# Another order on every engine, and other PSUM banks, in a four-layer graph network

## The chip, the cores and the metric

The kernel runs on one core of a Trainium2 chip. The metric is device time in microseconds of one execution; the time before is the median of three runs.

## The reference

The input `x` has 32 items of 512 nodes with 256 features, and all items share one 512 x 512 adjacency matrix `adj` (a sixteenth of it set). Four layers follow each other, each of the form `x = x + layer(relu(layernorm(x)))`, all in float32:

```python
# layer 0: dense attention over neighbours, one head of 256
e = leaky_relu((h @ W1) @ (h @ W2).T, 0.2); a = softmax(where(adj > 0, e, -1e12))
out = relu(a @ (h @ W3))
# layers 1 and 3: graph attention (GAT), 4 heads of 64
q = h @ W; e = leaky_relu(e_src[i] + e_dst[j], 0.2); a = softmax(where(adj > 0, e, -9e15))
out = elu(a @ q)
# layer 2: multi-head attention, 4 heads of 64, masked by adj, then @ Wo + bo and a layer norm
out = layernorm((softmax(mask(Q K^T / 8)) @ V) @ Wo + bo) * gamma + beta
```

## The kernel before

Nothing goes back to memory between the layers. The program is a software pipeline written out by hand: `first` does layer 0 and the front of layer 1 of item 0, then `slots` runs a list of *slots*. In one slot three items are in flight: item `a` is in layer 0 and the front of layer 1, item `b` (one older) in the rest of layer 1 and the front of layer 2, item `c` in the rest of layer 2 and in layer 3. Every engine (PE for matmuls and transposes, DVE, ACT, POOL, and SP for DMAs) has a `slot` function that lists its steps in the order in which that engine takes them, strictly one after the other. What one engine hands to another goes through a semaphore (`Signal`). There are 33 slots after `first`; in the first and in the last two of them one or two of the items are missing.

The names that matter here, all of them steps of one item:

- `transposed(w, layer, t)` on PE: the normalised activations `hn` are transposed, one of four row blocks, and ACT copies them out (`h_transposed`).
- `u_columns`, `scores0`, `v_rows`, `weights_transposed0`, `aggregate0`: layer 0 on PE; DVE does `masked_max0` and `lrelu0`, ACT the exponentials `exp0`; `relu0` (ACT), `residual0` (POOL) and the next statistics (DVE) close it.
- `q_rows`, `gat_max_across`, `gat_max_spread`, `gat_rows`: front of a GAT layer. `gat_rows_out` (DVE) leaves one row per head and block in `growT`; SP's `spread` writes it to DRAM and reads it back broadcast over 128 partitions (`r_loaded`), and only then can DVE make the weights, `gat_weights(w, g, h, *ts)`, that PE's `gat_aggregate(w, g, h)` needs with POOL's `gat_values`.
- `qk_columns`, `scores2`, `masked_max2`, `exp2`, `weights_transposed2`, `weights_out2`, `inverse_spread`, `aggregate2(w, p)`, `norm2`, `o_rows`, `o_out`: layer 2.
- `idle_turns(bank, count)`: matmuls of the identity into an unused bank, which stand in the thinly filled slots.

PSUM has eight banks; `BANK` says into which of them each stage writes. A stage may write a bank only when its former contents were copied out; where the order alone doesn't guarantee that, PE has a wait in its list, such as `masked0.wait(pe, a, 3)` ahead of `transposed(c, 3, 0)`. PE uses its array in three shapes: whole (128 x 128), half the columns (`gat_aggregate` and `aggregate2`, 128 x 64) and half the rows (`scores2`, 64 x 128).

## Time and profile before

| | |
|---|---|
| median of three runs | 2945.29 us (2944.38 to 2945.89) |
| profiled execution | span 2943.7 us; this plus 1.6 us is the median |
| instructions | 68275, of them 27732 matmuls and as many weight loads |
| granted TensorE clock, mean over the span | 0.997 of full speed |
| length of a full slot | 88.7 us |

The profile gives for each engine the time in which it was busy. Float32 matmuls appear as two instructions each, and they are pipelined: the start of one group to the start of the next says what a group costs, the duration of an instruction does not.

### The profile page before, as it was taken

The page shows a single profiled execution, that of the slowest core. Times are in us where ns is not written, and L with a number is a line of the kernel's source. Part 1 is how long each engine was busy: PE and PEld are TensorE (multiplying, and loading weights), DVE is VectorE, ACT ScalarE, POOL GpSimd, SP SyncE. Part 2 cuts the span into 40 slices and gives each one's busy share as a digit, 9 for nine tenths or more (in the row PEclk, how much of TensorE's full clock was granted, in tenths as well). Part 3 has the DMA queues.
Part 4 walks back from the last instruction along what each step waited for, and adds up shares of the span by engine and source line. Part 5 has one row for each costly group of instructions (what it writes and reads, how often), then busy time and mean ns, then how long its engine had stood idle before and what let it go on. Part 6 is the DMA issues. An engine that isn't in the chain of part 4 may idle for free.

```text
span 2943.7 us, 68275 instructions
## 1 busy us (share of the span) xinstructions
PE 2887.3 (98%) x27732; PEld 2034.8 (69%) x27732; DVE 2127.5 (72%) x5596; ACT 1682.3 (57%) x3554; POOL 827.8 (28%) x917
## 2 busy tenths in 40 slices
PE   7899999999999999999999999999999999999998
PEld 5566767666767666767667767667767667776766
DVE  5576787776787776877776877776877777877764
ACT  2555655655656655656655656656656656656543
POOL 2123222323222323222233232233222233222221
PEclk9999999999999999999999999999999999999999
DMA  3001011101011101011101011101011111011010
GB/s 102 22 23 45 27 41 45 44 23 45 23 44 45 44 23 44 23 44 44 38 30 44 23 45 44 37 30 44 23 45 44 34 33 40 28 37 37 17 36 30
DMA packets 58840, 109.89 MB, mean 37 GB/s; under 512 B 5568, under 2 KB 41408, under 8 KB 58528
## 3 DMA queue, kind: packets, MB, share of 16 engines
q1 hardware_dynamic: 58032, 104.61, 10.8%
q8 instruction: 220, 3.60, 0.5%
q0 software_dynamic: 496, 0.92, 0.3%
q14 instruction: 92, 0.75, 0.1%
HBM read 88.21 MB, written 17.30 MB: 36 GB/s over the span
## 4 chain that ended last, share of the span: by engine, by line
PE 77%; DVE 12%; POOL 6%; issue 2%; ACT 1%; SPq 0%; DMA 0%; POOLq 0%; DVEq 0%; ACTq 0%
PE ps L972 19%; PE ps L1080 11%; PE ps L1106 8%; PE ps L1115 8%; PE ps L978 8%; PE ps L1142 8%; PE ps L1029 8%; PE ps L958 4%; DVE stats L641 3%; POOL rstd L367 3%; POOL xc L417 3%; DVE pB L753 2%; PE ps L1017 2%; DVE nb L658 1%; DVE hn L829 1%
## 5 line engine op out<-in xcount | busy, mean ns | idle before, releaser
L389 POOL TENSOR_TENSOR qx<-qx,xc 128x512 f32<-128x512 f32 x128 | 163.7, 1279 | 869.4 <-ACT qx L529 869.4
L641 DVE BATCH_NORM_STATS2 stats<-xc 128x6 f32<-128x256 f32 x384 | 134.7, 413 | 328.6 <-POOL xc L399 264.1
L448 ACT ACTIVATE hn<-xc,nb,rstd 128x256 f32<-128x256 f32 x384 | 209.1, 592 | 163.9 <-DVE nb L658 160.7
L1080 PEld LDWEIGHTS ps<-vals,pA 128*64 128x64 f32 x8192 | 253.9, 138 | 54.6 <-issue 54.5
L972 PE MATMUL ps<-wgat,hT 128*128 128x264 f32 x1024 | 267.4, 395 | 1.8 <-ACT hT L457 1.8
L1080 PE MATMUL ps<-vals,pA 128*64 128x65 f32 x8192 | 266.4, 223 | 2.1 <-DVE pA L753 2.0
L1080 PE MATMUL ps<-vals,pB 128*64 128x65 f32 x8192 | 264.0, 223 | 0.3 <-DVE pB L753 0.2
L1080 PEld LDWEIGHTS ps<-vals,pB 128*64 128x64 f32 x8192 | 249.7, 138 | 16.8 <-issue 16.7
L457 ACT COPY hT<-ps 128x1024 f32<-128x1024 f32 x128 | 129.7, 1013 | 224.0 <-PE ps L958 219.8
L1106 PE MATMUL ps<-qx,qT 64*128 64x512 f32 x1024 | 249.8, 614 | 1.1 <-DVE hn L767 0.8
L364 POOL TENSOR_SCALAR rstd<-mv 128x4 f32<-128x4 f32 x160 | 75.0, 469 | 610.2 <-DVE mv L650 610.2
L1029 PE MATMUL ps<-vals,pB 128*128 128x256 f32 x1024 | 243.2, 381 | 1.1 <-ACT vals L469 1.1
L1142 PE MATMUL ps<-pX,vals 128*64 128x512 f32 x512 | 233.6, 599 | 2.3 <-DVE pA L806 2.3
L978 PE MATMUL ps<-hT,wqkvo 128*128 128x512 f32 x512 | 233.0, 598 | 0.8 <-ACT hT L457 0.8
L1008 PE MATMUL ps<-hT,qT 128*128 128x512 f32 x512 | 228.3, 599 | 1.1 <-ACT qT L463 1.1
L1029 PEld LDWEIGHTS ps<-vals,pB 128*128 128x128 f32 x1024 | 190.6, 191 | 38.9 <-issue 14.8
L972 PEld LDWEIGHTS ps<-wgat,hT 128*128 128x128 f32 x1024 | 179.5, 190 | 50.4 <-issue 24.9
L958 PE MATMUL ps<-ident,hn 128*128 128x128 f32 x1024 | 199.0, 280 | 11.9 <-ACT hn L448 11.1
L958 PEld LDWEIGHTS ps<-ident,hn 128*128 128x128 f32 x1024 | 132.3, 141 | 105.3 <-DVE rowmax L667 32.7
L367 POOL TENSOR_TENSOR rstd<-rstd,minus_half 128x4 f32<-128x4 f32 x160 | 192.5, 1203 | 13.3
L753 DVE SCALAR_TENSOR_TENSOR pA<-qT,gval,adjT 128x512 f32<-128x512 f32 x248 | 184.5, 785 | 6.7 <-DMA hT<-r_dram 6.5
L562 ACT ACTIVATE pX<-pX,negmax 128x512 f32<-128x512 f32 x256 | 183.4, 720 | 0.6 <-DVE negmax L797 0.6
(147 smaller groups left out, 6194.3 us busy)
## 6 DMA issues: line engine op xcount, KB each, us to landing
qT<-r_dram SPq DMA_DIRECT2D x64, 512.0 KB, 3.9
hT<-r_dram SPq DMA_DIRECT2D x64, 512.0 KB, 4.9
x_in<-in_x SPq DMA_DIRECT2D x32, 512.0 KB, 3.9
out_x<-xc SPq DMA_DIRECT2D x32, 512.0 KB, 3.0
pX<-in_adj SPq DMA_DIRECT2D x1, 1024.0 KB, 8.1
r_dram<-growT SPq DMA_DIRECT2D x64, 8.0 KB, 1.3
pX<-in_L_gnn_W SPq DMA_DIRECT2D x2, 256.0 KB, 5.2
pA<-in_L_gnn_a POOLq DMA_DIRECT2D x8, 64.0 KB, 8.8
```

The source lines that it names most:

```text
L367: nc.gpsimd.tensor_tensor(rstd[s][:, :], rstd[s][:, :], minus_half[:, :], ALU.pow).then_inc(rstd_ready[norm].sem, 1)
L641: last = nc.vector.bn_stats(stats[s][:, t, :], src[:, t, :])
L753: last = nc.vector.scalar_tensor_tensor(out=gat_p[s][h % 2][:, t, :], in0=row, scalar=gval[s][:, 1, t, h:h + 1], in1=adjT[:, t, :], op0=AL ...
L958: last = nc.tensor.transpose(ps[:, bank + k, t * P:(t + 1) * P], hn[s][:, t, k * P:(k + 1) * P], ident[:, :])
L972: last = nc.tensor.matmul(at, src[w.s][:, k, t * P:(t + 1) * P], wt[:, k, 0:width], start=(k == 0), stop=(k == KT - 1))
L978: last = nc.tensor.matmul(ps[:, bank + m, :], wt[:, k, m * P:(m + 1) * P], hT[w.s][:, k, :], start=(k == 0), stop=(k == KT - 1))
L1008: last = nc.tensor.matmul(ps[:, BANK[f"E{t}"], :], qT[s][:, k, t * P:(t + 1) * P], hT[s][:, k, :], start=(k == 0), stop=(k == KT - 1))
L1029: last = nc.tensor.matmul(rows_in(BANK["A"])[:, t, :], pB[s][:, t, j * P:(j + 1) * P], vals[s][:, j, 0:C], start=(j == 0), stop=(j == NT - 1))
L1080: last = nc.tensor.matmul(ps[lo:hi, BANK[f"G{g}.{h}"], t * DV:(t + 1) * DV], gat_p[s][h % 2][:, j, t * P + lo:t * P + hi], vals[s][:, j, h ...
L1106: last = nc.tensor.matmul(ps[:, BANK[f"S{p}.{t}"] + hh, :], qT[s][at, p, t * P:(t + 1) * P], kT[s][at, p, :], start=True, stop=True)
L1115: last = nc.tensor.transpose(ps[:, BANK[f"PT{h}.{t}"], j * P:(j + 1) * P], prob2[w.s][h][:, t, j * P:(j + 1) * P], ident[:, :])
L1142: last = nc.tensor.matmul(ps[hh * D:(hh + 1) * D, BANK[f"G2.{p}"], :], vals[s][:, j, h * D:(h + 1) * D], probT2[s][h][:, :, j * P:(j + 1) ...
```

## The change

All five `slot` lists and `first` are written anew. Nothing that is computed changes, and the number of instructions of each kind per item stays, but for the idle turns.

- The slot is cut at another place. `slot` now gets `z, a, b, c, d, e`, where `z` is the item after `a`. The statistics of `z` for layer 0 (`statistics(z, 0)`, `mean_and_variance(z, 0)`, `deviation(z, 0)`) run one slot early; `gat_values(a, 1)` and `gat_exp(a, 1)` run at the end of the slot of `a` and not at the start of the next; some transposes of layer 2 and the last head of layer 3 run in the next slot. There are 34 slots in place of 33.
- PE: `gat_aggregate(c, 3, 0)` and `(c, 3, 1)` stand around the first four `scores2`; `transposed(a, 0, t)` no longer alternate with `o_rows`, nor `transposed(a, 1, t)` with `v_rows(b, 2, t)`; `v_rows(a, 0, 0)` comes after all `scores0`; the wait `masked0.wait(pe, a, 3)` ahead of `transposed(c, 3, 0)` goes; the waits inside `aggregate0` and `aggregate2` move into the list.
- The banks of nearly all stages change.
- `first`: `aggregate0` stands behind the transposition of the adjacency matrix, the bias row and `poison`, with `pe.wait_ge(setup_ok, 6)` ahead of it. `shift_of_norm(a, 0)` of item 1 waits for POOL's `deviation(z, 0)` ahead of the first `gat_weights`.
- Idle turns: 191 calls' worth in place of 175.
- `x_in` has two buffers in place of three; the load of item n + 2 is the last thing of SP's slot and not the first.
- The semaphores `stats_ok` and `var_eps` are folded into `mv_ready` and `rstd_ready`, which now count to 2.

PE's list, whose order the text speaks of, cut to its core:

```diff
-                aggregate2(c, 0)
-                gnorm[3].wait(pe, d, 4); weights_transposed2(c, 3, 0); weights_transposed2(c, 2, 2)
...
-                pT2_dve[2].wait(pe, c, 2); inverse_spread(c, 1); aggregate2(c, 1); gat_aggregate(b, 1, 0)
-                o_rows(c, 0); transposed(a, 0, 0); o_rows(c, 1); transposed(a, 0, 1); o_rows(c, 2)
...
-                masked0.wait(pe, a, 3)
...
-                transposed(c, 3, 0); v_rows(a, 0, 1); transposed(c, 3, 1)
...
+                v2_ready.wait(pe, c); weights_transposed2(c, 0, 2); rT_out[1].wait(pe, b)
+                weights_transposed2(c, 0, 3); weights_transposed2(c, 1, 2); weights_transposed2(c, 2, 0)
+                weights_transposed2(c, 2, 1); pT2_dve[0].wait(pe, c, 3); weights_transposed2(c, 1, 3)
+                weights_transposed2(c, 2, 2); pT2_act[1].wait(pe, c, 3); weights_transposed2(c, 2, 3)
+                gat_aggregate(d, 3, 3); pT2_act[0].wait(pe, c); pT2_dve[1].wait(pe, c); aggregate2(c, 0)
+                pT2_dve[2].wait(pe, c); weights_transposed2(c, 3, 0); weights_transposed2(c, 3, 1)
+                weights_transposed2(c, 3, 2); weights_transposed2(c, 3, 3); inverse_spread(c, 0); inverse_spread(c, 1)
+                pT2_dve[3].wait(pe, c, 2); pT2_act[3].wait(pe, c, 2); aggregate2(c, 1); inv_ready.wait(pe, c)
+                gat_aggregate(b, 1, 0); o_rows(c, 0); o_rows(c, 1); o_rows(c, 2); o_rows(c, 3); transposed(a, 0, 0)
+                transposed(a, 0, 1); transposed(a, 0, 2); transposed(a, 0, 3); gat_aggregate(b, 1, 1)
+                o_ready.wait(pe, c); gat_aggregate(b, 1, 2); u_columns(a, 0); u_columns(a, 1)
...
+                gat_aggregate(b, 1, 3); scores0(a, 0); gnorm[1].wait(pe, b, 3); scores0(a, 1); scores0(a, 2)
+                scores0(a, 3); gnorm[1].wait(pe, b, 4); v_rows(a, 0, 0)
...
+                transposed(c, 3, 0); v_rows(a, 0, 1); transposed(c, 3, 1); transposed(c, 3, 2); transposed(c, 3, 3)
...
+                gat_aggregate(c, 3, 0); scores2(b, 0, 0); kT_ready.wait(pe, b, 2); scores2(b, 0, 1); scores2(b, 1, 0)
+                masked2[0].wait(pe, b, 2); scores2(b, 0, 2); gat_aggregate(c, 3, 1); masked2[0].wait(pe, b, 4)
+                transposed(a, 1, 0); transposed(a, 1, 1); transposed(a, 1, 2); transposed(a, 1, 3)
...
+                pT2_dve[0].wait(pe, b); gat_aggregate(c, 3, 2); gat_rows(a, 1); weights_transposed2(b, 1, 1)
```

DVE's list from the middle of the slot to its end, and the start of the next one:

```diff
+                mean_and_variance(z, 0); gat_rows_out(c, 3); weights_out0(a, 3); gat_weights(c, 3, 0, 0, 1, 2, 3)
+                gat_weights(c, 3, 1, 0, 1, 2); statistics(a, 1); mean_and_variance(a, 1); masked_max2(b, 0, 0, 0)
...
+                gat_weights(c, 3, 3, 0); weights_out2(b, 0, 1); gat_rows_out(a, 1)
...
+                gat_weights(d, 3, 3, 1); weights_out2(c, 0, 2); shift_of_norm(a, 0); gat_weights(d, 3, 3, 2, 3)
+                weights_out2(c, 1, 3); gat_out(d, 3, 0); gat_norm(d, 3, 2); weights_out2(c, 2, 1); gat_norm(d, 3, 3)
+                inverse_sums2(c, 0); gat_weights(b, 1, 0, 0); weights_out2(c, 2, 3); gat_weights(b, 1, 0, 1)
+                inverse_sums2(c, 1); weights_out2(c, 3, 1); weights_out2(c, 3, 2); gat_weights(b, 1, 0, 2, 3)
+                gat_weights(b, 1, 1, 0); norm2(c, 0); gat_weights(b, 1, 1, 1); gat_out(d, 3, 1)
+                gat_weights(b, 1, 1, 2); norm2(c, 1); gat_weights(b, 1, 1, 3); gat_weights(b, 1, 2, 0, 1, 2, 3)
```

PE's `first`, from the transposes of layer 0's weights:

```diff
+                weights_transposed0(a, 1); weights_transposed0(a, 2); pT0_act.wait(pe, a); weights_transposed0(a, 3)
+                pT0_act.wait(pe, a, 2); adjacency(); pT0_dve.wait(pe, a); bias_row(); poison()
+                pe.wait_ge(setup_ok, 6); aggregate0(a, 0); aggregate0(a, 1); aggregate0(a, 2); aggregate0(a, 3)
```

## Rows read from the trace of the kernel before

**Rows 1.** The page: busy time by engine, and one DMA row

```profile
PE 2887.3 (98%) x27732; PEld 2034.8 (69%) x27732; DVE 2127.5 (72%) x5596; ACT 1682.3 (57%) x3554; POOL 827.8 (28%) x917
...
hT<-r_dram SPq DMA_DIRECT2D x64, 512.0 KB, 4.9
```

**Rows 2.** Windows: one full slot, the last two slots (busy, clock, DMA)

```profile
1448.50:1537.20 88.70, 88.32 (x856) 62.00 (x856) 65.96 (x175) 52.49 (x111) 25.66 (x28) 1.00 0.12 37
...
2796.30:2879.00 82.70, 75.30 (x827) 53.15 (x823) 55.46 (x133) 37.68 (x83) 18.84 (x22) 0.96 0.10 33
2879.00:2943.70 64.70, 51.69 (x565) 42.70 (x561) 28.49 (x62) 17.36 (x35) 11.77 (x13) 0.97 0.10 34
```

**Rows 3.** Timeline of PE, a full slot: start, us, instructions, [idle before]

```profile
1448.51 2.09 PE L1080 MATMUL ps<-vals,pA 128*64 128x65 f32 x64
1450.53 1.16 PE L972 MATMUL ps<-wgat,hT 128*128 128x264 f32 x4
...
1473.39 1.26 PE L1126 MATMUL ps<-ident,qx 128*128 128x128 f32 x8
1474.70 0.61 PE L1142 MATMUL ps<-pB,vals 128*64 128x512 f32 x1
...
1491.19 2.09 PE L1080 MATMUL ps<-vals,pA 128*64 128x65 f32 x64
1493.11 2.04 PE L1080 MATMUL ps<-vals,pB 128*64 128x65 f32 x64
1495.08 7.13 PE L1008 MATMUL ps<-hT,qT 128*128 128x512 f32 x16
1502.50 0.41 PE L958 MATMUL ps<-ident,hn 128*128 128x128 f32 x2 [0.29 <-ACT hn L448]
...
1537.19 2.09 PE L1080 MATMUL ps<-vals,pA 128*64 128x65 f32 x64
```

**Rows 4.** Timeline of PE: first, and the slot after it

```profile
34.70 5.34 PE L1029 MATMUL ps<-vals,pB 128*128 128x256 f32 x24
...
51.35 1.09 PE L958 MATMUL ps<-ident,hn 128*128 128x128 f32 x8 [0.50 <-DVE adjT L912]
...
65.28 2.09 PE L1080 MATMUL ps<-vals,pA 128*64 128x65 f32 x64 [1.57 <-DVE pA L753]
...
93.28 3.33 PE L1029 MATMUL ps<-vals,pB 128*128 128x256 f32 x8
...
136.30 0.61 PE L1142 MATMUL ps<-pX,vals 128*64 128x512 f32 x1 [2.25 <-DVE pA L806]
```

**Rows 5.** Waits of PE: total us, times, longest us

```profile
PE ps L958 <- ACT hn L448: 11.1, 33, 1.6
```

**Rows 6.** Timeline of ACT, one slot later than Rows 3

```profile
1562.45 0.59 ACT L573 COPY pX<-ps 128x512 f32<-128x512 f32 x1
...
1590.34 0.60 ACT L448 ACTIVATE hn<-xc,nb,rstd 128x256 f32<-128x256 f32 x1 [1.72 <-DVE nb L658]
```

**Rows 7.** Timeline of DVE, the slot before the last one

```profile
2847.58 0.75 DVE L753 SCALAR_TENSOR_TENSOR pA<-qT,gval,adjT 128x512 f32<-128x512 f32 x1 [6.54 <-DMA hT<-r_dram]
```

**Rows 8.** Timeline of DVE, same slot as Rows 6

```profile
1563.05 2.70 DVE L753 SCALAR_TENSOR_TENSOR pA<-qT,gval,adjT 128x512 f32<-128x512 f32 x4
...
1615.74 1.11 DVE L753 SCALAR_TENSOR_TENSOR pA<-qT,gval,adjT 128x512 f32<-128x512 f32 x1
```

**Rows 9.** Timeline of SP's queue, a row written and read back

```profile
1552.48 0.32 SPq L322 DMA_DIRECT2D r_dram<-growT  x1
1554.49 0.32 SPq L326 DMA_DIRECT2D qT<-r_dram  x1
```

**Rows 10.** Timeline of DVE in first

```profile
39.08 0.16 DVE L908 TENSOR_REDUCE part_any<-row_any 128x1 f32<-128x4 f32 x1
...
49.01 2.28 DVE L912 COPY adjT<-ps 128x2048 f32<-128x2048 f32 x1
```

**Rows 11.** Timeline of PE, idle turns of the last slot

```profile
2895.89 14.56 PE L966 MATMUL ps<-ident 128*128 128x128 f32 x128 [1.32 <-DVE hn L829]
```

More of the change, by code:

```diff
@@ L341, in _ @@
                 sp.sem_inc(x_stored[s], 16)
-                if s > 0:
+                if 0 < s < X_SETS:
                     load(Work(s), 0)
-            for n in range(B + 2):
-                slot(*[Work(n - d) if 0 <= n - d < B else None for d in range(SETS)], more=n + SETS < B)
+            slots(first, slot)
             for s in range(SETS):
@@ new lines, in slot @@
+                masked2[0].wait(pe, b, 6); scores2(b, 1, 1); masked2[1].wait(pe, b, 2); scores2(b, 0, 3)
+                q_rows(a, 1, 0); q_rows(a, 1, 1)
+                if a is None and b is not None:
+                    idle_turns(4, 5)
+                masked2[0].wait(pe, b, 8); scores2(b, 1, 2); qx_ready[1].wait(pe, a); scores2(b, 1, 3)
+                gnorm[3].wait(pe, c, 2); q_rows(a, 1, 2); q_rows(a, 1, 3); masked2[1].wait(pe, b, 4); v_rows(b, 2, 0)
+                masked2[1].wait(pe, b, 6); weights_transposed2(b, 0, 0); v_rows(b, 2, 1); gat_max_across(a, 1)
@@ L1224, in factors_transposed @@
+                v_rows(b, 2, 2); v_rows(b, 2, 3); gat_max_spread(a, 1); masked2[1].wait(pe, b, 8)
+                weights_transposed2(b, 0, 1); weights_transposed2(b, 1, 0)
+                if b is None and c is not None:
+                    idle_turns(5, 8)
+                pT2_dve[0].wait(pe, b); gat_aggregate(c, 3, 2); gat_rows(a, 1); weights_transposed2(b, 1, 1)
             def factors_transposed():
```

319 lines of the change are left out of this document (128 added, 191 removed), and 16 rows, old and new, of the table BANK.

## The prediction

> **What bounds the kernel.** I read the page first: PE is busy for 98% of the span, DVE for 72%, ACT for 57%, and HBM traffic is small [rows 1]. So PE's list is the kernel, and other engines matter only where PE waits for them. Cut into slots, the trace gives a full slot of 88.7 us with 88.3 us of PE in it; the last two slots take 82.7 and 64.7 us, and there PE is busy for 75.3 and 51.7 us, part of it idle turns [rows 2]. The timeline of PE gives the period more exactly: the `gat_aggregate` with which scores are followed starts at 1448.51 and again at 1537.19, 88.68 us later [rows 3]. Slots 2 to 31 are alike, 30 of them; from the first `aggregate2` (136.30, [rows 4]) to that of slot 32 (2796.3, [rows 2]) it is 2660 us, 88.67 each, and 88.6 without the stretch at half clock just behind 136.30. The rest is the way in (136.3 us) and the way out (147.4 us). I cost the change against these three parts.
>
> Idle time is the smaller half of what a slot loses; the other half hides in the distance between starts. Three places in a slot:
>
> - The wait ahead of `transposed(c, 3, 0)`: 0.29 us in this slot, 11.1 us over 33 times [rows 3, 5]. It ends with ACT's normalisation, which starts at 1590.34 in the next slot [rows 6], 88.7 us after the time when PE wants it. The pipeline must start again behind it, some 0.1 us more (my estimate; below nothing it can't be).
> - The eight transposes of `inverse_spread` take 1.31 us from their start to that of `aggregate2(c, 1)` [rows 3], where eight others take 1.09 us with their whole pipeline delay [rows 4]. They and `aggregate2` wait for ACT's copies, the last of which but two starts at 1562.45 [rows 6]. Worth 0.2 to 0.4 us.
> - A change of array shape. A head followed by another head takes 1.92 us (1491.19 to 1493.11); followed by whole-array matmuls it takes 2.02 us (1448.51 to 1450.53) [rows 3]. So 0.10 us at each border.
>
> **What the change removes.** PE's matmuls are the same, so the period can only lose the first two items and what small hand-overs cost. The `masked0` wait is gone, because T3 no longer shares a bank with E2. Between the end of `o_rows(c)` and `transposed(c, 3, 0)` PE now has four transposes, three heads, two `u_columns`, four `scores0` and one `v_rows`: 0.9 + 5.9 + 3.5 + 7.0 + 0.9 and borders, 18.6 us, against 18.0 us in which ACT was 0.3 us late. The chain that must be done in it (output bias, statistics, POOL's deviation, normalisation, gamma, residual, statistics again, normalisation) is as long as before, so it is on time by some 0.3 us at the least, and by over 1 us where DVE's shorter queue ahead of it helps. `inverse_spread` now stands behind all four `weights_transposed2(c, 3, t)`, with ACT's `inverse_columns` done by then; only the copy of (3, 3), 0.59 us [rows 6], has to fit under the 0.9 us of the eight transposes, and does, just. Gain of both and of the hand-overs of interleaved transposes: between 0.4 us (the idle time and the lower end of the second) and 1.0 us a slot. I take 0.8.
>
> **What it adds.** Borders: I count nine stretches of other shapes per slot before, 18 borders; after, eight stretches, but one of them goes from half columns to half rows and back, 18 borders again. At 0.10 us each this is nothing; if a change between the two half shapes cost double, plus 0.2 us.
>
> New tight places on DVE, each by the durations of the rows:
>
> - `gat_aggregate(c, 3, 0)` stands right behind `qk_columns`, some 10.7 us after `gat_rows_out(c, 3)` and not 20 us. The way through DRAM took 6.54 us where DVE had nothing else to do [rows 7]; four weights take 2.70 us [rows 8]. Together 9.3 us: 1.4 us of slack. DVE then makes three weights of head 1 (2.0 us), the statistics (1.8 us) and two `masked_max2` (1.2 us), 14.3 us after `gat_rows_out`, and `scores2(b, 0, 2)` wants them at about 15.4.
> - In the first half of the slot `gat_weights(b, 1, 0, 0)` now comes some 7 us after `gat_rows_out(a, 1)`. For layer 1 the write takes 2.0 us before the reads are issued [rows 9], and the read back 4.9 us [rows 1]: 7.3 us with the second issue, and DVE waits up to 1 us. Behind it in DVE's queue stand `weights_out2(c, 2, 3)`, `inverse_sums2(c, 1)`, `weights_out2(c, 3, 1)` and `(3, 2)`, which `aggregate2(c, 1)` needs, and `norm2(c, 1)`, which `o_rows` needs. By the sum of their durations `norm2(c, 1)` is done 0.4 us before PE has ended `gat_aggregate(b, 1, 0)`.
>
> I charge 0.2 us for these. Net, 0.6 us a slot: a period of 88.0 us, times 30, minus 18 us. The bounds for the period are 87.6 (all of it gained) and 88.6 (gained and given back).
>
> **The way in.** `aggregate0` of item 0 ran from 32.0 to 39.9 us (its last three blocks start at 34.70 [rows 4]) while DVE did `neighbours` (to 39.2) and waited; the adjacency copy came at 49.01 for 2.28 us [rows 10]. Now `aggregate0` waits for that copy. DVE reaches it at about 39.9 (the row of neighbours is ready some 0.8 us sooner, at 38.4, then three short hand-overs of 0.5 us), so `aggregate0` starts at 42.3 and ends at 49.2, 9.3 us later. Two things come back: the statistics need not wait for the bias row (1.5 us), and the transposes at 51.35 no longer wait 0.5 us for the copy [rows 4]; about 1 us more of slack there goes. That leaves 6.8 us. The second `first` cost: PE is nearly empty from 36.6 to 42.3. After such a stretch, in slot 1, eight matmuls took 3.33 us where 24 took 5.34 [rows 4], the clock granted being half (1.2 GHz); I take 2 us for it, 0 to 3.4. Then DVE waits for POOL's `deviation(z, 0)` ahead of the first weights, 1.8 us. In all the first head starts at 75.9 and not 65.28. But slot 1 is not full: it lost 2.25 us in its last wait alone [rows 4], over 5 us more in shorter ones, and at two places the clock. Item 0's chain through layer 2 is shorter in the new order, since no interleaved work stands in it. Walking both lists to the first `aggregate2`, I find the new one at 142 to 144 and not at 136.3: plus 6.5 us, between 2 (slot 1 takes up the delay) and 12 (it takes up none of it).
>
> **The way out.** In slot 32 the order has the second half of layer 2 closer together, worth 2 to 3 us of the 7 us idle there [rows 2]. In the last slot 76 idle turns now stand between `o_ready` and `transposed(c, 3, 0)`, 152 instructions; 128 took 14.4 us [rows 11], so they take 17.1, and normalised rows that were ready when the turns ended must now wait 1.8 us. Nine more turns before head 0 of layer 3 cost 0.9; fewer before heads 1 and 3 give back 2. The extra slot adds no work, only the tail of the last. In all minus 2 us, between minus 5 and plus 3.
>
> **Input buffers and semaphores.** The load of item n + 2 is issued when `residual0` of item n has read its buffer, and its statistics run 70 us later; a load lands in about 4 us. Nothing, and nothing below nothing, unless it meets the read back of `spread`, which is issued before it. The folded semaphores take no instruction away.
>
> **The sum.** 2943.7 - 18 + 6.5 - 2 = 2930.2 us of span; plus 1.6 us as before it is 2931.8. I say 2932 us, 0.45% faster. A difference of 0.2% (5.9 us) is about what the measurement can tell.
>
> **Rivals.**
>
> 1. *DVE gives it all back: no change.* The gain in the period is 0.2 to 0.3 us and the way in costs what I say: minus 7 + 6.5 - 2, 2943 us. For it: the slack of 0.4 us ahead of `o_rows` is smaller than any error of my sums. Against: the waits on DVE that I find are single ones. 0.2.
> 2. *POOL blocks DVE: slower.* One `gat_weights` took 1.11 us and not 0.74 at 1615.74, when POOL made `gat_values` [rows 8]. Before, this met one instruction in a slot. In the new order the `gat_values(a, 1)` at the slot's end meet two or three of `gat_weights(·, 3, 3, ·)`, and `gat_residual(d, 3, 1)` meets `gat_weights(b, 1, 0, ·)`. At 0.37 us each, or at up to POOL's own 0.6 to 1.3 us, DVE is 1 us late in the queue before `norm2(c, 1)`; from 0.4 us on PE waits one for one, with 1.0 us the period is 88.9, and the time 2943.7 + 9 + 6.5 - 2 + 1.6, 2959 us. The Trainium skill, "SBUF — State Buffer", section "Who interferes with whom", says that a DVE instruction with two SBUF inputs contends with a GpSimd instruction that reads SBUF, and that the one which comes second is fully blocked; by that rule this rival is the likely one in each such meeting, and the trace agrees in the one row at 1615.74. 0.17.
> 3. *More is gained.* All hand-overs go and the way in is caught up in slot 1: period 87.6, minus 30 + 2 - 4, 2913 us. 0.08.
> 4. *My forecast*, 2922 to 2940 us: 0.55.
>
> Faster by over 0.2% is my forecast nearly whole and rival 3, 0.62; within 0.2% is rival 1 and the edges, 0.2; slower 0.18. The range reaches from rival 3's inner side to the inner side of rival 2, 2917 to 2952; the forecast's own is 2922 to 2940.
>
> **What would show it.** The distance between two `aggregate2(c, 0)` in full slots: 88.0, right; above 88.5, wrong. `transposed(c, 3, 0)` without a wait for ACT, `inverse_spread` to `aggregate2(c, 1)` in 1.0 us. PE's waits would name DVE's `norm2` or `gat_weights` (rivals 1 and 2), and `gat_weights` of over 0.8 us would show rival 2. In `first`, `aggregate0` at 42 us and not 32, the first `aggregate2` at 143, some of `aggregate0` at half clock. From the last full slot to the end, 2 us less than before. I am wrong if a second wait that my walk missed recurs in each slot, since each 0.2 us of it is 6 us.

## The result, and the profile after

| | before | after |
|---|---|---|
| median, both measured on one chip | 2944.84 us (2943.82 to 2945.89, 4 runs) | 2929.99 us (2927.78 to 2932.78, 4 runs) |
| profiled span | 2943.7 us | 2926.0 us |
| granted clock, mean | 0.997 | 0.996 |

The ratio is 0.9948, with an interval of 0.9933 to 0.9962: faster by 0.5%. Forecast were 2932 us, so the total is right. Its parts are not. They are read from one profiled execution each, which was the fastest of its four for the kernel after (2927.78 us), so they add up to 2.2 us less than its median. Cut at the first `aggregate2` of slot 2's item and of slot 32's, as the prediction did:

| part | before | forecast | after |
|---|---|---|---|
| way in, to the first `aggregate2` | 136.3 | +6.5 | 147.6 (+11.3) |
| 30 slots | 2660.0 (88.67 each) | -18 (88.07) | 2627.9 (87.60 each; -32.1) |
| way out | 147.4 | -2 | 150.5 (+3.1) |
| span | 2943.7 | 2930.2 | 2926.0 (-17.7) |

Part 1 of the page of the kernel after, against [rows 1]:

```profile
PE 2872.5 (98%) x27764; PEld 2045.5 (70%) x27764; DVE 2134.2 (73%) x5596; ACT 1667.6 (57%) x3554; POOL 790.4 (27%) x917
```

The windows of the kernel after: the way in, one full slot from `aggregate2` to `aggregate2`, the way out (columns as in [rows 2]):

```profile
0.00:147.60 147.60, 115.73 (x722) 81.23 (x723) 72.96 (x193) 52.57 (x109) 32.51 (x50) 0.94 0.21 54
1461.15:1548.71 87.56, 87.56 (x860) 62.05 (x858) 66.46 (x174) 52.09 (x112) 24.23 (x28) 1.00 0.12 39
2775.50:2926.00 150.50, 129.07 (x1428) 102.47 (x1424) 82.50 (x196) 54.11 (x114) 28.32 (x30) 0.97 0.08 27
```

PE is busy for the whole full slot: 87.56 of 87.56 us, before 88.32 of 88.70 [rows 2]. PE is idle for 22% of the way in and for 14% of the way out, with the idle turns counted as busy.

The timeline of PE after, same full slot, with the two places at which [rows 3] lost time, and further down the two ends:

```profile
43.30 8.86 PE L1018 MATMUL ps<-vals,pB 128*128 128x256 f32 x32 [2.64 <-DVE adjT L902]
...
77.75 3.60 PE L1069 MATMUL ps<-vals,pA 128*64 128x65 f32 x64 [5.67 <-DVE pA L746]
81.28 1.09 PE L948 MATMUL ps<-ident,hn 128*128 128x128 f32 x8
...
1466.49 1.04 PE L1115 MATMUL ps<-ident,qx 128*128 128x128 f32 x8
1467.45 0.64 PE L1128 MATMUL ps<-pB,vals 128*64 128x512 f32 x1
...
1486.96 7.13 PE L998 MATMUL ps<-hT,qT 128*128 128x512 f32 x16
1493.93 1.03 PE L962 MATMUL ps<-w,hT 128*128 128x256 f32 x4
1494.79 0.38 PE L948 MATMUL ps<-ident,hn 128*128 128x128 f32 x2
...
2805.03 8.73 PE L956 MATMUL ps<-ident 128*128 128x128 f32 x62 [4.33 <-DVE hn L760]
2813.59 1.04 PE L948 MATMUL ps<-ident,hn 128*128 128x128 f32 x8
...
2876.43 17.24 PE L956 MATMUL ps<-ident 128*128 128x128 f32 x152 [1.32 <-DVE hn L822]
2893.50 1.04 PE L948 MATMUL ps<-ident,hn 128*128 128x128 f32 x8
```

Start to start, the eight `inverse_spread` transposes (1466.49) take 0.96 us and not 1.31 as in the slot of [rows 3] (1.23 in most slots, see below), and the sixteen `scores0` (1486.96) take 6.97 us and not 7.42 as in [rows 3], since nothing behind them waits. At the ends, the first head (77.75) waits 5.67 us for DVE's weights and is then made at half clock, 3.53 us to the next start and not 2. In slot 32 the idle turns (2805.03) stand behind a wait of 4.33 us and run to 2813.59, in part at half clock.

### The profile page after: what moved, and what is told of

Its sections match the earlier page's. It is cut to its first block, busy times and chain, and to the rows that moved or that the text cites. A ratio compares the mean times of both kernels' runs of the same rounds, so it can differ in the third digit from the quotient of the medians.

```text
span 2926.0 us, 68155 instructions
## 1 busy us (share of the span) xinstructions
PE 2872.5 (98%) x27764; PEld 2045.5 (70%) x27764; DVE 2134.2 (73%) x5596; ACT 1667.6 (57%) x3554; POOL 790.4 (27%) x917
## 4 chain that ended last, share of the span: by engine, by line
PE 94%; DVE 2%; DMA 1%; ACT 1%; issue 1%; POOL 0%; SPq 0%; POOLq 0%; DVEq 0%; ACTq 0%
PE ps L962 20%; PE ps L1069 17%; PE ps L968 11%; PE ps L1095 8%; PE ps L998 8%; PE ps L1128 8%; PE ps L1104 8%; PE ps L1018 8%; PE ps L948 4%; PE ps L1007 2%; PE ps L1115 1%; PE ps L956 1%; DMA hT<-r_dram 1%; DVE pA L746 0%; DVE stats L634 0%
## 5 line engine op out<-in xcount | busy, mean ns | idle before, releaser
L746 DVE SCALAR_TENSOR_TENSOR pA<-qT,gval,adjT 128x512 f32<-128x512 f32 x248 | 202.6, 856 | 208.8 <-DMA hT<-r_dram 208.1
L384 POOL TENSOR_TENSOR qx<-qx,xc 128x512 f32<-128x512 f32 x128 | 174.6, 1364 | 647.5 <-ACT qx L524 647.5
L443 ACT ACTIVATE hn<-xc,nb,rstd 128x256 f32<-128x256 f32 x384 | 202.5, 595 | 140.4 <-DVE nb L651 140.4
L359 POOL TENSOR_SCALAR rstd<-mv 128x4 f32<-128x4 f32 x160 | 37.2, 232 | 880.7 <-DVE mv L643 880.7
L962 PE MATMUL ps<-wgat,hT 128*128 128x264 f32 x1024 | 255.0, 393 | 0.4 <-ACT hT L452 0.4
L962 PEld LDWEIGHTS ps<-wgat,hT 128*128 128x128 f32 x1024 | 186.9, 190 | 74.5 <-ACT hT L452 23.5
L968 PE MATMUL ps<-hT,wqkvo 128*128 128x512 f32 x512 | 224.9, 592 | 0.0
L372 POOL TENSOR_TENSOR vals<-qx,gval 128x256 f32<-128x256 f32 x256 | 153.8, 623 | 216.2 <-ACT gval L515 216.2
L746 DVE SCALAR_TENSOR_TENSOR pB<-hT,gval,adjT 128x512 f32<-128x512 f32 x256 | 186.6, 760 | 0.0
L362 POOL TENSOR_TENSOR rstd<-rstd,minus_half 128x4 f32<-128x4 f32 x160 | 181.9, 1137 | 13.4 <-POOL rstd L359 0.2
```

The lines of the kernel that those rows point to most:

```text
L362: nc.gpsimd.tensor_tensor(rstd[s][:, :], rstd[s][:, :], minus_half[:, :], ALU.pow).then_inc(rstd_ready[norm].sem, 1)
L443: nc.scalar.activation(hn[s][:, t, :], src[:, t, :], ACT.Identity if norm == "in" else ACT.Relu, bias=nb[s][:, t:t + 1], scale=rstd[s][:, ...
L746: last = nc.vector.scalar_tensor_tensor(out=gat_p[s][h % 2][:, t, :], in0=row, scalar=gval[s][:, 1, t, h:h + 1], in1=adjT[:, t, :], op0=AL ...
L962: last = nc.tensor.matmul(at, src[w.s][:, k, t * P:(t + 1) * P], wt[:, k, 0:width], start=(k == 0), stop=(k == KT - 1))
L968: last = nc.tensor.matmul(ps[:, bank + m, :], wt[:, k, m * P:(m + 1) * P], hT[w.s][:, k, :], start=(k == 0), stop=(k == KT - 1))
```

## Where a full slot gained: distances between starts

A group's cost is the distance from its start to the next start. I summed these by step (worked out from the PE records of each trace; "the rest" holds `aggregate2`, heads, `scores2`, columns, `aggregate0` and small ones; kernels 1 to 4 are the first four experiments below). The figures are medians over the 29 full slots behind the first one, so a column can miss its sum by 0.02 us:

| us in a slot | before | after | 1: one `v_rows` | 2: two `v_rows` | 3: inverse | 4: relu |
|---|---|---|---|---|---|---|
| `inverse_spread` | 1.23 | 0.97 | 1.23 | 1.23 | 1.05 | 1.23 |
| `scores0` to T3 or `v_rows` | 7.42 | 6.97 | 6.97 | 6.97 | 7.42 | 6.97 |
| all `transposed` | 4.05 | 3.74 | 4.50 | 3.89 | 4.05 | 3.89 |
| `weights_transposed0` | 1.84 | 1.84 | 1.84 | 2.67 | 1.84 | 2.31 |
| `to_row` (all projections to rows) | 18.35 | 17.99 | 18.35 | 18.38 | 18.35 | 19.14 |
| the rest | 55.70 | 56.06 | 55.70 | 55.70 | 55.70 | 55.70 |
| slot | 88.59 | 87.57 | 88.59 | 88.83 | 88.41 | 89.22 |
| mean of all 30 | 88.67 | 87.60 | 88.67 | 88.90 | 88.48 | 89.30 |

The slot of [rows 3] is not the usual one: its `inverse_spread` takes 1.31 us, as in 6 of the 29, and 1.23 in the others. Timeline of PE of the kernel before, the next slot:

```profile
1562.07 1.26 PE L1126 MATMUL ps<-ident,qx 128*128 128x128 f32 x8
1563.29 0.61 PE L1142 MATMUL ps<-pB,vals 128*64 128x512 f32 x1
```

The gain in such a slot is 1.02 us: 0.26 (inverse) + 0.45 (ahead of T3) + 0.16 (inside T3, by experiments 2 and 4) + 0.15 for all changes of shape and order together. The last is the difference of larger ones: the other `transposed` and `to_row` give 0.51 us, the rest takes 0.36 back; which move made it was not tried. The mean falls by 1.07 us and not 1.02, chiefly because the first of the 30 slots took 90.33 us before: a stretch of it ran at half clock, and no slot of the kernel after has one there. Window of the kernel before:

```profile
137.20:140.40 3.20, 3.20 (x10) 1.21 (x8) 0.47 (x2) 1.70 (x7) 1.43 (x4) 0.50 0.89 283
```

That is 1.7 of the 32.1 us.

## Experiments

### 1. The kernel before, one `v_rows` ahead of T3

```diff
+                v_rows(a, 0, 1)
                 masked0.wait(pe, a, 3)
...
-                transposed(c, 3, 0); v_rows(a, 0, 1); transposed(c, 3, 1)
+                transposed(c, 3, 0); transposed(c, 3, 1)
```

> The kernel before, with one step of the change alone: `v_rows(a, 0, 1)` (two matmuls, 0.9 us) moved ahead of the wait for `masked0` and of `transposed(c, 3, 0)`, so that ACT's normalised rows have 0.9 us more time. Theory A (the prediction's first item): the idle time of 0.29 us in front of T3 goes and the pipeline need not start again, 0.4 us a slot in all, period 88.67 to 88.25 us, times 30 makes minus 12 us, about 2933 us; PE's wait sum at that line falls from 11.1 us to under 2. Rival B: behind T3 the next link of the same chain (ACT's copy of T3, the query rows of layer 3, DVE's row maxima) is late by what was gained, a wait of some 0.3 us appears there, and the time stays within 3 us of the kernel before.

Measured: 2944.63 us, ratio 0.9999 (0.999 to 1.0009). Theory A falls, and rival B's place for the wait too. The idle time in front of T3 is gone from the waits, yet the time is the same. Its timeline of PE shows where it went:

```profile
1501.13 1.03 PE L972 MATMUL ps<-w,hT 128*128 128x256 f32 x4
1501.99 1.43 PE L958 MATMUL ps<-ident,hn 128*128 128x128 f32 x6
1503.26 1.03 PE L972 MATMUL ps<-w,hT 128*128 128x256 f32 x4
```

Six transposes (three blocks) take 1.27 us to the next start, where six without a wait take 0.65. No wait is printed, since the group hides what lies between its instructions. ACT starts the first three blocks at 1500.83, 1501.86 and 1502.35; the third is 8.2 us behind the start of `scores0`, as before, and it sets the end. So moving one piece of work ahead of a wait moved the idle time behind it.

### 2. The kernel before, two `v_rows` ahead of T3

```diff
+                v_rows(a, 0, 1); v_rows(a, 0, 2)
                 masked0.wait(pe, a, 3)
...
+                transposed(c, 3, 0); transposed(c, 3, 1)
+                transposed(c, 3, 2); v_rows(a, 0, 3); transposed(c, 3, 3)
```

> The kernel before, with two `v_rows` of item a (steps 1 and 2, 1.7 us of PE) ahead of `transposed(c, 3, 0)`, and the other one ahead of `transposed(c, 3, 3)`. With one of them moved, the wait ahead of T3's first block was gone (`scores0` to the next matmul 6.97 us and not 7.42), but six transposes then took 1.27 us and not 0.65, and the period stayed at 88.67 us. Theory A: ACT normalises the four blocks one behind the other, and it is the third block that sets the end of T3 (0.14 us of loss in the kernel before, behind the 0.45 us at the first); with two `v_rows` ahead all of it is covered, the period falls by 0.59 us to 88.08, and 30 slots make minus 17.7 us, about 2927.5 us. Rival B: the chain behind T3 (ACT's copy of it, query rows, row maxima) or `v_rows`' own outlet sets a wait that takes it back, and the time stays within 4 us of the kernel before.

Measured: 2951.50 us, ratio 1.0021 (1.0011 to 1.003), slower. Both losses at T3 are gone as theory A said (6.97 us, and 0.16 off the transposes), and rival B takes back more than that. Timeline of PE and, last line, the waits of PE (total, times, longest):

```profile
1506.22 0.82 PE L958 MATMUL ps<-ident,hn 128*128 128x128 f32 x6
1506.87 1.03 PE L972 MATMUL ps<-w,hT 128*128 128x256 f32 x4
1507.74 0.38 PE L958 MATMUL ps<-ident,hn 128*128 128x128 f32 x2
1507.96 0.60 PE L1017 MATMUL ps<-ident,pA 128*128 128x128 f32 x4
1509.22 1.16 PE L972 MATMUL ps<-wgat,hT 128*128 128x264 f32 x4 [0.67 <-ACT hT L457]
```

```profile
PE ps L972 <- ACT hT L457: 21.6, 34, 1.2
```

T3's last block comes at 1507.74, ACT copies T3 out in 1.0 us, and `q_rows` waits for it, 0.67 us in this slot and 21.6 us over 34 times. The work that covered this copy is what I had moved ahead of T3. In this order of PE there is no room: what is put in front of the wait is missing behind it.

### 3. The kernel before, ACT's inverse columns sooner

```diff
-                weights_out2(c, 3, 1); inverse_columns(c, 1); weights_out2(c, 3, 3); inverse_out(c, 0)
+                inverse_columns(c, 1); weights_out2(c, 3, 1); weights_out2(c, 3, 3); inverse_out(c, 0)
```

> The kernel before, with ACT's `inverse_columns(c, 1)` ahead of the copy `weights_out2(c, 3, 1)` and not behind it, 0.6 us sooner. In the kernel after, with ACT in this order and PE's too, the eight `inverse_spread` to `aggregate2(c, 1)` take 0.96 us; before 1.31. Theory A (the prediction's second item: PE waits inside the spread for ACT's columns): 0.2 to 0.35 us a slot, period 88.35 to 88.45, minus 6 to minus 10 us. Rival B: the copy (3, 1) and then (3, 3) come 0.4 us later instead, `aggregate2(c, 1)` waits for them, and the time is the same within 3 us, or up to 3 us longer.

Measured: 2939.63 us, ratio 0.9978 (0.9969 to 0.9987). Theory A's mechanism, at the lower edge of its size: one swap in ACT's list takes the eight transposes from 1.23 to 1.05 us, the slot from 88.59 to 88.41, 0.18 us, and the whole by 5.9 us. This part of the change works alone; the other 0.08 us, to 0.97, comes with the new order.

### 4. The kernel before, POOL's residual kept away from DVE's shift

The trace of the kernel before has 160 shifts of a norm, each of 128 x 4 elements. 130 take 0.15 to 0.17 us, and 30, one in each full slot (1411.76, 1500.44, 1589.02 and so on), take 1.22 or 1.23. Timeline of DVE, ACT and POOL of the kernel before:

```profile
1500.44 1.23 DVE L658 SCALAR_TENSOR_TENSOR nb<-mv,rstd 128x4 f32<-128x4 f32 x1 [0.32 <-POOL rstd L367]
...
1501.76 0.60 ACT L448 ACTIVATE hn<-xc,nb,rstd 128x256 f32<-128x256 f32 x1 [1.72 <-DVE nb L658]
...
1498.83 1.57 POOL L367 TENSOR_TENSOR rstd<-rstd,minus_half 128x4 f32<-128x4 f32 x1
1500.38 1.26 POOL L389 TENSOR_TENSOR qx<-qx,xc 128x512 f32<-128x512 f32 x1
```

The shift starts 0.06 us behind POOL's residual and ends with it; ACT's rows for T3 wait for just this shift. The same places of the kernel after:

```profile
1491.61 0.16 DVE L651 SCALAR_TENSOR_TENSOR nb<-mv,rstd 128x4 f32<-128x4 f32 x1 [0.45 <-POOL rstd L362]
...
1491.87 1.59 ACT L443 ACTIVATE hn<-xc,nb,rstd 128x256 f32<-128x256 f32 x3
...
1490.54 1.04 POOL L362 TENSOR_TENSOR rstd<-rstd,minus_half 128x4 f32<-128x4 f32 x1
1494.05 1.46 POOL L384 TENSOR_TENSOR qx<-qx,xc 128x512 f32<-128x512 f32 x1 [2.48 <-ACT qx L524]
```

The residual is now released by an `elu_relu` that stands behind three of ACT's rows. So this step was moved in ACT's list of the kernel before. A second one moved with it: `elu_exp(b, 1, 1)` stood behind the first of ACT's rows and now stands ahead of it, as in the kernel after.

```diff
-                elu_relu(b, 1, 0); elu_min(b, 1, 1); elu_relu(b, 1, 1); normalised(c, 3, 0)
-                elu_exp(b, 1, 1); normalised(c, 3, 1); normalised(c, 3, 2); normalised(c, 3, 3); exp0(a, 0)
+                elu_relu(b, 1, 0); elu_min(b, 1, 1); elu_exp(b, 1, 1); normalised(c, 3, 0)
+                normalised(c, 3, 1); normalised(c, 3, 2); elu_relu(b, 1, 1); normalised(c, 3, 3); exp0(a, 0)
```

> The kernel before, with one step of ACT moved: `elu_relu(b, 1, 1)`, which releases POOL's `gat_residual(b, 1, 1)`, stands behind `normalised(c, 3, 2)` and not ahead of `normalised(c, 3, 0)`. In the kernel before, that residual runs on POOL from 1500.38 to 1501.64, and DVE's shift of item c's norm (128 x 4 elements), which starts at 1500.44, takes 1.23 us; in other places such a shift takes 0.16. ACT's normalised rows wait for it, and `masked_max0(a, 2)`, which T3 also waits for, stands behind it on DVE. In the kernel after, the shift takes 0.16. Theory A (POOL's residual held DVE, and that is what PE's loss at T3 comes from): the shift takes 0.16 us, ACT's rows come 1.07 us sooner, the 0.45 us ahead of T3's first block and the 0.14 us inside T3 go, the period is 88.68 - 0.59 = 88.09 us, and 30 slots make minus 17.7 us, about 2928 us. Rival B: it is the chain's sum and not this instruction; ACT has other work in between, and less than 0.2 us a slot is gained. Rival C: the later residual delays DVE's `gat_out(b, 1, 1)` and so item b's layer 2, and the period grows.

Measured: 2966.69 us, ratio 1.0066 (1.0049 to 1.0083), slower. Theory A's mechanism holds: all 160 shifts take 0.15 to 0.17 us, the chain from DVE's bias addition to ACT's first row takes 16.1 us (1495.69 to 1511.80) and not 17.2, and both losses at T3 are gone (6.97 us, and 0.16 off the transposes). ACT's second and third row come 0.5 us sooner still, since `elu_exp` is out of their way; by the numbers the 1.07 us of the shift cover 0.45 + 0.16 without that, but it wasn't tried apart. Rival C holds too, by another way than I wrote, and costs more. Timeline of DVE, ACT and PE of this kernel:

```profile
1511.54 0.16 DVE L658 SCALAR_TENSOR_TENSOR nb<-mv,rstd 128x4 f32<-128x4 f32 x1 [0.32 <-POOL rstd L367]
...
1515.28 0.75 DVE L777 SCALAR_TENSOR_TENSOR xc<-qT,minus_one,qx 128x512 f32<-128x512 f32 x1 [1.07 <-POOL qx L389]
...
1516.41 0.72 ACT L479 ACTIVATE pA<-pA,negmax 128x512 f32<-128x512 f32 x1 [2.01 <-DVE negmax L689]
...
1517.27 0.66 PE L1017 MATMUL ps<-ident,pA 128*128 128x128 f32 x4 [0.48 <-ACT pA L479]
1518.17 1.16 PE L972 MATMUL ps<-wgat,hT 128*128 128x264 f32 x4 [0.24 <-ACT hT L457]
```

DVE now waits 1.07 us for the residual ahead of `gat_out`; the row maxima of item a's softmax stand behind that in its queue, ACT's exponentials behind those, PE's `weights_transposed0` behind those, and ACT's copy of T3 behind the first exponential. The kernel after differs here in more than this one step: ACT copies T3 ahead of `exp0`, and PE has two `v_rows` and half of `q_rows` between T3 and `weights_transposed0`. Its trace shows no such wait in a full slot; which of these moves takes it away was not tried.

### 5. One idle turn between two shapes, and one inside whole-array work

Both on the kernel after, in full slots alone.

```diff
-                masked2[0].wait(pe, b, 2); scores2(b, 0, 2); gat_aggregate(c, 3, 1); masked2[0].wait(pe, b, 4)
+                masked2[0].wait(pe, b, 2); scores2(b, 0, 2)
+                idle_turns(0, 1)
+                gat_aggregate(c, 3, 1); masked2[0].wait(pe, b, 4)
```

> The kernel after, with one more idle turn (two whole-array matmuls of 128 rows each, 0.22 us by the rate of the turns in the last slot, 17.24 us for 152) between the last `scores2(b, 0, 2)` and `gat_aggregate(c, 3, 1)` in each full slot. These two stretches have different partial array shapes and now touch. The prediction's rule, 0.10 us at each border between two shapes: one border becomes two, so the period grows by 0.22 + 0.10 = 0.32 us, from 87.56 to 87.88. Theory B, drawn from the two traces: what costs is a separate stretch of another shape between whole-array work, 0.3 us for each, and a change between two partial shapes inside it costs 0.1: the period grows by 0.22 + 0.3 - 0.1 = 0.42 us or more, to 87.98 or beyond. Theory C, all of it lies in slack of other engines: nothing, but PE shows no wait there, so this is not likely.

```diff
+                idle_turns(2, 1)
                 aggregate0(a, 0); gat_max_across(c, 3); ...
```

> The kernel after, with one more idle turn (two whole-array matmuls of 128 rows) ahead of `aggregate0(a, 0)`, inside whole-array work, in each full slot: the control for the turn between two shapes. If PE is the bound all through the slot, the period grows by the turn's own 0.22 us, 87.56 to 87.78. If somewhere behind it PE waits for another engine, it grows by less. The difference between this kernel's period and that of the turn between shapes is the price of cutting a stretch in two: 0.10 us by the prediction's rule, 0.2 or more by the rule that a separate stretch costs 0.3.

Measured (one run each, so by the period of most slots): 87.99 us with the turn between two shapes, 87.79 with the other, 87.57 without. The turn costs 0.22 us, and cutting a stretch in two 0.20 us more. The timeline of PE with the turn between:

```profile
1530.38 3.82 PE L1095 MATMUL ps<-qx,qT 64*128 64x512 f32 x16
1534.13 0.49 PE L956 MATMUL ps<-ident 128*128 128x128 f32 x2
1534.55 2.09 PE L1069 MATMUL ps<-vals,pB 128*64 128x65 f32 x64
```

The 3.75 us from `scores2` to what follows is the same with the turn and without it (there a head follows, 1520.89 to 1524.64). So leaving one partial shape costs the same whether whole-array work or the other partial shape comes next; what the merged stretch saves is the way back in from whole-array work, 0.20 us at this place. It is less at others: in the kernel after, eight transposes ahead of a head take 0.97 us to its start (1476.46 to 1477.43), and 0.88 by the rate of six with whole-array work behind them, so 0.09. The prediction's rule of 0.10 at every border is too low by 0.10 here, and its "nothing" for eight stretches in place of nine left out one way back in.

### 6. How much room DVE has ahead of `o_rows`

```diff
                 gat_weights(b, 1, 1, 2)
+                nc.vector.scalar_tensor_tensor(out=spare[i][:, :], in0=gat_r[b.s][1], ...)   # 128 x 512
                 norm2(c, 1)
```

> The kernel after, with one more instruction of the `gat_weights` form (128 x 512, into a buffer that nobody reads) on DVE ahead of `norm2(c, 1)` in each full slot, 0.66 to 0.74 us of DVE. The prediction gives `norm2(c, 1)` 0.4 us of slack ahead of `o_rows`. Theory A (that slack is all there is): the period grows by 0.26 to 0.34 us, to 87.85, and PE shows a wait for DVE ahead of the first matmuls of `o_rows`. Rival B: the work in DVE's queue ahead of it, or POOL, leaves more room than the durations show, and the period stays at 87.56.

> The kernel after, with two more instructions of the `gat_weights` form on DVE ahead of `norm2(c, 1)` in each full slot, 1.33 to 1.48 us of DVE. Theory A (0.4 us of slack, then PE waits one for one): the period grows by 0.9 to 1.1 us, to about 88.55, which is where rival 1 of the prediction puts it. Rival B: it grows by less, since PE's wait there takes up others, or DVE catches up. This also prices rival 2 of the prediction, in which POOL costs DVE 1 us in that queue.

Measured: periods (means of 30 slots) of 87.80 (+0.20) and 88.42 (+0.82); 2937.22 and 2955.43 us, one run each. Timeline of DVE and PE with one more, and the waits of PE with two more:

```profile
1478.09 0.75 DVE L844 SCALAR_TENSOR_TENSOR spare<-qT,gval,adjT 128x512 f32<-128x512 f32 x1
1478.75 0.69 DVE L816 TENSOR_TENSOR qT<-ps,qx 128x512 f32<-128x512 f32 x1
...
1477.33 2.04 PE L1076 MATMUL ps<-vals,pA 128*64 128x65 f32 x64
1479.49 3.72 PE L969 MATMUL ps<-wqkvo,qT 128*128 128x256 f32 x16
```

```profile
PE ps L969 <- DVE qT L816: 24.6, 31, 0.9
```

The added instruction moves `norm2` by 0.66 us; the head ahead of `o_rows` takes 2.16 us and not 1.96. So the room is 0.66 - 0.20 = 0.46 us, and beyond it PE waits one for one (1.32 - 0.46 = 0.86, measured 0.82). The prediction had 0.4. It is enough for what rival 2 described, which does happen; timeline of DVE and POOL of the kernel after:

```profile
1550.36 1.84 DVE L746 SCALAR_TENSOR_TENSOR pA<-qT,gval,adjT 128x512 f32<-128x512 f32 x1 [0.68 <-DMA hT<-r_dram]
...
1550.38 1.27 POOL L384 TENSOR_TENSOR qx<-qx,xc 128x512 f32<-128x512 f32 x1 [6.89 <-ACT qx L524]
```

One `gat_weights` takes 1.84 us there and not 0.74. In the 30 slots that begin at 235.22 and later it takes 1.31 to 1.87 us in six; in the other 24 it takes 0.75 and the next one 1.16 to 1.22, by how its start (set by a DMA's landing) falls to POOL's. The 0.46 us of room are what the added instructions found with this going on: DVE's `norm2` makes PE wait once in the whole run (0.9 us in total, from PE's waits). PE shows no wait for the held instruction in a full slot.

### 7. The way in

```diff
-                pT0_act.wait(pe, a, 2); adjacency(); pT0_dve.wait(pe, a); bias_row(); poison()
-                pe.wait_ge(setup_ok, 6); aggregate0(a, 0); aggregate0(a, 1); aggregate0(a, 2); aggregate0(a, 3)
+                pT0_act.wait(pe, a, 2); aggregate0(a, 0); aggregate0(a, 1); pT0_dve.wait(pe, a, 2)
+                aggregate0(a, 2); aggregate0(a, 3); agg0_norm.wait(pe, a, 4); adjacency(); bias_row(); poison()
```

DVE's list in `first` follows suit (`inverse_sum0` ahead of `weights_out0(a, 3)`, statistics ahead of `poison` and `adjacency_out`).

> The kernel after, with only the way in of item 0 in the old order: `aggregate0` ahead of the adjacency, and statistics and `inverse_sum0` of DVE accordingly. In the kernel after, `aggregate0` of item 0 starts at 43.3 and the first `aggregate2` at 147.6 us, 11.3 us later than before. Theory A (the prediction's term for the way in, of which slot 1 takes up little): `aggregate0` at about 32 again, the first head at 68 to 71 and not 77.75, the first `aggregate2` 5 to 9 us earlier, and the time 5 to 9 us less, about 2923 us. Rival B: slot 1's own chains (POOL's deviation of item 1, ACT, the missing idle turns) set the first `aggregate2`, which then moves by under 2 us, and the time stays at 2928 to 2930.

Measured: 2922.05 us, ratio to the kernel before 0.9923 (0.9908 to 0.9937). Theory A: `aggregate0` at 35.24, first head at 69.77, first `aggregate2` at 139.37, 8.2 us sooner. The full slots are the same (87.60).

```diff
+                if c is None and b is not None:
+                    idle_turns(1, 20)
```

> The kernel after, with 20 idle turns in bank 1 at the start of slot 1, some 4.4 us of TensorE work at full clock in the stretch from 70.6 to 80.8 us, in which PE waits for DVE's first weights and the granted clock is the lower of its two levels (1.2 GHz); the first head takes 3.60 us there and not 2. Theory A: the turns fill idle time (5.67 us ahead of the first head) and the head runs at 2.4 GHz: minus 1.5 us at the first `aggregate2`. Rival B: the turns themselves are made at the lower clock, take 8.7 us, and delay the head: plus 2 to 3 us. Rival C: the first `aggregate2` is set by another chain than PE's and does not move.

Measured: first `aggregate2` at 148.63, 2931.56 us, one run. The turns keep the clock up: the head at 78.41 takes 2.02 us to the next start and not 3.53. But the first `aggregate2` isn't sooner. It falls at 147.5 to 147.9 us in three kernels with this way in (the profiled kernel after is one) and at 150.4 to 151.0 in three others, and the granted clock goes with it: the three late ones have one more stretch at half clock, near 112 us, and so has the kernel with the turns. Windows of the kernel with the turns and, below, of the kernel after:

```profile
109.60:112.80 3.20, 3.20 (x11) 2.56 (x10) 0.47 (x1) 1.27 (x3) 1.86 (x1) 0.50 0.03 5
109.60:112.80 3.20, 3.20 (x19) 2.81 (x18) 1.12 (x6) 1.92 (x4) 1.20 (x1) 1.00 0.00 0
```

From the first head to the first `aggregate2` it is 69.9 to 70.0 us in the three early kernels, 71.3 to 71.4 in the three late ones and 70.2 with the turns: 1.1 us less than in those that lost the clock at the same place. This speaks for theory A and against rival C, but it is one run. Inconclusive.

### 8. The way out

```diff
-                scores0(a, 3); gnorm[1].wait(pe, b, 4); v_rows(a, 0, 0)
+                scores0(a, 3)
                 if a is None and b is not None:
                     idle_turns(0, 31)
+                gnorm[1].wait(pe, b, 4); v_rows(a, 0, 0)
...
-                    idle_turns(7, 76)
+                    idle_turns(7, 60)
```

> The kernel after, with the way out changed alone: in slot 32 the 31 idle turns stand ahead of the wait for `gnorm[1]` of item 31 and not behind it, and the last slot has 60 idle turns and not 76. In the kernel after, PE waits 4.33 us there (2805.03) and then makes 6.8 us of turns, while the normalised rows for T3 are ready at 2808.8, 4.7 us ahead of T3; in the last slot T3 comes 1.6 to 3.6 us after its rows are ready, 16 turns are 1.8 us. Theory A (the way out is set by turns that stand in PE's queue behind a wait): minus 4.5 us in slot 32 and minus 1.8 us in slot 33, about 6 us in all, 2924 us. Rival B: T3 comes sooner but what follows it (ACT's copies, the rows through DRAM, the heads of layer 3) runs at the half clock or waits for a transfer, and under 3 us is left.

Measured: 2925.01 us, ratio 0.9926 (0.991 to 0.9943); the way out takes 144.3 us and not 150.5. Timeline of PE in slot 32:

```profile
2804.23 7.19 PE L956 MATMUL ps<-ident 128*128 128x128 f32 x62
2811.25 0.82 PE L948 MATMUL ps<-ident,hn 128*128 128x128 f32 x6
2812.46 0.44 PE L948 MATMUL ps<-ident,hn 128*128 128x128 f32 x2 [0.38 <-ACT hn L443]
```

T3 is now set by ACT's rows. From the slot's first `aggregate2` to the end of T3 it is 33.6 us and not 39.0: 5.3 us. The next 79.9 us become 77.7, 2.2 us for the 16 turns; but then the last stretch takes 33.0 us and not 31.6, at a granted clock of 0.90 and not 0.97, and the same 341 matmuls keep PE busy 1.6 us longer. Windows of this kernel and, below, of the kernel after:

```profile
2890.44:2923.40 32.96, 21.72 (x341) 19.81 (x339) 16.45 (x32) 6.19 (x12) 5.47 (x7) 0.90 0.14 50
```

```profile
2894.38:2926.00 31.62, 20.09 (x341) 18.18 (x339) 16.46 (x32) 6.20 (x12) 5.47 (x7) 0.97 0.15 51
```

So the lower clock takes 1.3 of the 2.2 us in this run. That the missing turns caused it is not shown, and two other kernels speak against it. The same stretch of experiment 5's second kernel, which has all 76 turns, and below it of experiment 9's, which has 60:

```profile
2900.92:2934.80 33.88, 21.44 (x341) 19.54 (x339) 16.53 (x32) 6.19 (x12) 5.47 (x7) 0.90 0.15 48
```

```profile
2879.47:2911.50 32.03, 20.09 (x341) 18.18 (x339) 16.45 (x32) 6.20 (x12) 5.48 (x7) 0.97 0.16 51
```

Here the clock at the end falls with 76 turns and stays with 60, so it varies between these kernels for a reason that the runs don't show. The way out of five kernels that have it as in the kernel after takes 150.0, 150.5 and 151.0 us in three and 152.7 and 152.8 in two; 144.3 is below them all.

### 9. All of it

```diff
-                deviation(a, 1); deviation(z, 0); gat_values(a, 1)      # POOL, first
+                deviation(a, 1); gat_values(a, 1); deviation(z, 0)
...
+                if c is None:                                           # DVE, slot
+                    gat_weights(b, 1, 0, 0, 1, 2, 3)
```

with the edits of 7 (without the turns) and 8.

> The kernel after with its full slots unchanged and both ends mended. Way in: `aggregate0` of item 0 ahead of the adjacency, as in the kernel before (alone it gave 8.2 us at the first `aggregate2`); POOL makes item 0's layer-1 weights' values ahead of the deviation of item 1, and in slot 1 DVE makes the first weights of head 0 at once. Way out: idle turns ahead of the wait for `gnorm[1]` in slot 32, and 60 turns in the last slot and not 76 (alone 6.2 us from the first `aggregate2` of slot 32 to the end). Theory A, the parts add up: 2930 - 8 - 6, and 1 to 2 us from the first weights, which now come sooner: 2914 us, 1.05% less than before. Rival B: the two at the ends each uncover the next link, above all the first weights, for which DVE waits for POOL and for the row through DRAM in any case: nothing from the third part, 2916 us. Rival C: the earlier `gat_values` delay item 1's deviation and so its layer 0 in slot 1, and the way in is longer by 1 to 2 us: 2918.

Measured: 2911.56 us (2910.55 to 2913.35), ratio 0.9886 (0.9871 to 0.9901) to the kernel before: 34.0 us less, and 18.4 less than the kernel after (2929.99 us, beside a median of the kernel before that was 0.7 us lower); between the profiled spans it is 14.5 us. It beats both kernels. The first head comes at 67.20, 2.6 us sooner than in 7, but the first `aggregate2` at 139.74, where it was (139.37). So the third part brought nothing in this execution, the time of rival B. Its reason is open: a stretch from 100.6 to 103.8 us ran at a granted clock of 0.50 here and of 1.00 in 7. The full slots take 87.6 us, the way out 143.3.

## Why the prediction was right, point by point

- **The period.** Forecast 88.0, measured 87.6: sign and places right, size too small. The gain of 0.8 a slot that I took for idle time and hand-overs was 0.87 (0.26 + 0.45 + 0.16); the 0.29 us that the wait shows was less than half of what T3 cost (0.61), the rest being hidden between starts and inside a group. The charge of 0.2 us for DVE was nothing that the trace shows: PE shows no wait for DVE in any full slot. The changes of shape and order gave 0.15 and not nothing, and 0.05 is the stretch at half clock that the first of the 30 slots had before. Over 30 slots that is 14 us that I left out. My 1.31 us for `inverse_spread` was the slower kind of slot, and the 1.09 beside it a duration and not a distance; the range of 0.2 to 0.4 holds the measured 0.26 all the same.
- **The step behind T3 was wrong in its reason.** I wrote that the chain to T3's rows "is as long as before" and counted 18.6 us of cover against 18.0. It is shorter: from DVE's bias addition to ACT's first row it took 17.2 us before (1484.57 to 1501.76) and 15.2 after (1476.66 to 1491.87). 1.07 of the 2.0 us is the shift that POOL's residual held up, which experiment 4 took away on the kernel before. The rest lies, by the two traces, in POOL's `rstd` (1.57 us at 1498.83, while DVE's `gat_out` ran from 1498.77, and 1.04 at 1490.54), 0.53, and in a `masked_max0` that stood ahead of the mean and variance, 0.37; these two weren't tried alone. I had seen this contention at one `gat_weights` [rows 8] and looked for it only where the new order would add it, not on the chain that set the wait [rows 6], where the old order had it in each slot.
- **The way in.** Forecast +6.5, measured +11.3, inside the bound of 12. `aggregate0` at 43.30 (42.3 forecast) and its loss at half clock (8.86 us and not 7.2) were as said, the first head at 77.75 was 1.9 us later than said. (The 6.8 us in that sum are too many by its own terms: 9.3 - 1.5 - 0.5 - 1 is 6.3.) The term that failed is slot 1: I let it take up 4.1 us of the head's delay, and it took up 1.2: from head to `aggregate2` 69.9 us, before 71.0 [rows 4]. In the three late kernels that experiment 7 names, with one more stretch at half clock, the way in is longer than before by 14.1 to 14.7 us, outside the bound. The first part of experiment 7 gives 8.2 us back.
- **The way out.** Forecast -2, measured +3.1, just past the upper bound of 3. The 76 turns cost about what I said. What I missed is that `gnorm[1].wait(pe, b, 4)` now stands ahead of 31 turns: a wait of 4.33 us and then 8.6 us of turns in a row (7.0 at full clock; I wrote 6.8 in the expectation of experiment 8), where ACT's last row, from 2808.20 to 2808.78, was ready 4.8 us before T3. I had costed the turns by their number and not by what they stand behind. Experiment 8 gives 5.3 us back there.
- **Rivals.** Rival 1 was wrong: the slack of 0.46 us holds. Rival 2's mechanism is there: in the 30 slots all `gat_weights` together take 0.5 to 1.8 us longer than at 0.74 each (before, 0.4), in no wait of PE; its threshold of 0.4 us and "one for one" beyond it are right. Its sum is not: 0.6 us past the threshold, on top of 88.0, is 88.6 or 88.7 and not 88.9, which makes about 2950 us and not 2959. With 1.32 us added, experiment 6 measured 88.4. By the rule of the Trainium skill, "SBUF — State Buffer", section "Who interferes with whom", each such meeting blocks the instruction that comes second, so the rule would have pointed to a gain as well as to a loss. The traces agree at 1500.44 before (DVE second by 0.06 us and held) and at 1112.32 after (POOL second by 0.23 us, 1.66 us and not 1.27). The meeting at 1550.36 after doesn't show it: DVE's start stands 0.02 us ahead of POOL's there, and DVE was the one held. Rival 3's period of 87.6 is the measured one; I gave it 0.08.
- **Why the total came out right.** Errors of -14, +4.8 and +5.1 us add up to -4. This is luck, not accuracy: each part came out at or near the outer end of its own bounds, the way out past it.
- Input buffers: DVE waits for an input once in the whole run, 4.9 us at its very start, and in no full slot; this part wasn't tried alone.
